# The output's bias in the dense recurrent stage: a one-row product on TensorE in place of GpSimd's addition

## What is computed

```python
def _gru_cell(x, h, wih, whh, bih, bhh):
    gi = x @ wih.T + bih
    gh = h @ whh.T + bhh
    i_r, i_z, i_n = jnp.split(gi, 3, axis=-1)
    h_r, h_z, h_n = jnp.split(gh, 3, axis=-1)
    r = jax.nn.sigmoid(i_r + h_r)
    z = jax.nn.sigmoid(i_z + h_z)
    n = jnp.tanh(i_n + r * h_n)
    return (1.0 - z) * n + z * h
...
h = jax.nn.relu(node_features @ node_proj_w.T + node_proj_b)
for l in range(L):
    ...
    h = _gru_cell(agg, h, gru_wih[l], gru_whh[l], gru_bih[l], gru_bhh[l])
    h = jax.nn.relu(h)
return h @ out_w.T + out_b
...
x = _layernorm(x + _L2_gnn_ref(x, ...), axis=-1)
```

## Time and profile before

| | us |
|---|---|
| median of 3 runs | 5060.44 |
| lowest and highest run | 5043.36, 5065.11 |
| the profiled execution | 5037.14 |
| its span, first to last instruction | 5035.4 |
| the dense recurrent stage | about 2290 to 3155 of the span |

### The profile page before, as it was taken

One profiled execution on the slowest core, in us unless ns is written; L12 is line 12 of the kernel. 1 busy time (PEld: TensorE's weight loads), 2 busy tenths in 40 slices (PEclk: granted clock), 3 DMA queues, 4 the chain that ended last, 5 costly groups with the idle time before them and its releaser, 6 DMA issues. The chain is left out here.

```text
span 5035.4 us, 61135 instructions
## 1 busy us (share of the span) xinstructions
PE 3692.6 (73%) x15176; PEld 2317.9 (46%) x15176; DVE 3382.6 (67%) x10490; ACT 2054.5 (41%) x4190; POOL 3267.5 (65%) x2884
## 2 busy tenths in 40 slices
PE   6677777774688852226999998699798758777975
PEld 4466666663344531113555554344344427665322
DVE  7878778875455543333888888465576649887964
ACT  1455555553233321115777776122222212222742
POOL 2367767774788737775888888554268867463557
PEclk9888888887899965558999999799898979899988
DMA  2344444442333321212333333333333327685863
GB/s 88 103 123 124 124 119 117 127 116 85 76 88 92 85 55 55 60 53 73 128 125 129 121 129 113 99 108 106 88 99 96 96 85 242 195 184 131 272 202 117
DMA packets 422550, 582.11 MB, mean 116 GB/s; under 512 B 69157, under 2 KB 191708, under 8 KB 422268
## 3 DMA queue, kind: packets, MB, share of 16 engines
q1 hardware_dynamic: 361660, 495.02, 31.5%
q0 software_dynamic: 54912, 83.37, 7.6%
q10 hardware_dynamic: 5696, 0.55, 0.1%
HBM read 370.70 MB, written 211.65 MB: 116 GB/s over the span
## 5 line engine op out<-in xcount | busy, mean ns | idle before, releaser
L1225 PE MATMUL ps<-big,Whh 128*128 128x512 f32 x1176 | 540.0, 595 | 33.7 <-DVE big L1243 30.4
L710 PE MATMUL ps<-W2b,hid 128*128 128x128 f32 x1568 | 260.2, 335 | 242.5 <-DVE rN L903 169.3
L1636 PE MATMUL ps<-big,We 128*128 128x512 f32 x800 | 373.0, 621 | 1.3 <-DVE agg L1810 1.1
L710 PEld LDWEIGHTS ps<-W2b,hid 128*128 128x128 f32 x1568 | 243.0, 243 | 263.4 <-issue 262.3
L1225 PEld LDWEIGHTS ps<-big,Whh 128*128 128x128 f32 x1176 | 211.8, 190 | 254.2 <-issue 251.4
L633 POOL TENSOR_TENSOR rsq<-veq,mhalf 128x8 f32<-128x8 f32 x106 | 178.9, 1688 | 201.7 <-DVE veq L942 201.4
L1784 DVE SCALAR_TENSOR_TENSOR big<-r2N,zN 128x512 f32<-128x512 f32 x400 | 258.1, 700 | 33.7 <-issue 24.1
L1258 POOL TENSOR_TENSOR big<-big 128x512 f32<-128x512 f32 x196 | 252.1, 1307 | 43.8 <-ACT big L1252 43.8
L739 ACT ACTIVATE hid<-ps 128x512 f32<-128x512 f32 x98 | 58.6, 598 | 537.4 <-PE ps L702 537.4
L599 POOL DMA_INDIRECT me<-node_tab,ix x208 | 218.9, 1052 | 70.4 <-issue 53.6
L606 POOL DMA_INDIRECT meta<-me,rank_ix x208 | 220.0, 1058 | 62.3 <-issue 61.4
(11 more groups left out here) (396 smaller groups left out, 11222.9 us busy)
## 6 DMA issues: line engine op xcount, KB each, us to landing
xN<-x_tab SPq DMA_DIRECT2D x196, 256.0 KB, 2.9
x_tab<-zN SPq DMA_DIRECT2D x189, 256.0 KB
h_tab<-yN SPq DMA_DIRECT2D x124, 256.0 KB
krow<-key_row SPq DMA_DIRECT2D x100, 256.5 KB
agg<-in_xt SPq DMA_DIRECT2D x98, 256.0 KB
agg<-x_tab SPq DMA_DIRECT2D x98, 256.0 KB
x_tab<-yN SPq DMA_DIRECT2D x93, 256.0 KB
xN<-in_x SPq DMA_DIRECT2D x65, 256.0 KB
```

Of the source, the lines that this page charges most:

```text
L710: last = nc.tensor.matmul(OUT0[:, spans[j]], hid1[g % 2][:, c, spans[j]], W2b[:, c, :], start=(c == 0), stop=(c == 1))
L1225: last = nc.tensor.matmul(bank[:, :], Whh[:, l, c * D:(c + 1) * D], h, start=True, stop=not both)
L1636: last = nc.tensor.matmul(MS[:, :], We[:, l * NTYPE + t, :], masked[g % 2][:, t, :], start=(t == 0), stop=(t == NTYPE - 1))
```

## The change

The output's bias is no longer added to x by GpSimd. For each tile of 128 rows, TensorE first forms a one-row product, 1 x 128 ones by the bias row, in the PSUM region of the output, and the product with Wo accumulates on it. VectorE's residual adds PSUM and `xR` directly. SP's second load of x into `xR` now waits for the residual that read it (`rd`), no longer for GpSimd's addition (`xbd`).

```diff
-            tpd, cpd, projd, h0d, xbd, tp1d, cp1d, yd, rd = ph.sems(9)
+            tpd, cpd, projd, h0d, tp1d, cp1d, yd, rd = ph.sems(8)
...
                     def load_again(i, q):
                         for u in range(2):
-                            free(sp, xbd, i, u=u)
+                            free(sp, rd, i, u=u)
                             sp.dma_start(xR[u], group(x2_tab, 2 * i + u)).then_inc(xagain[u], 16)
...
-                    def add_bias(i, q):
-                        for u in range(2):
-                            pool.wait_ge(xagain[u], 16 * i + 16)
-                            free(pool, rd, i, u=u)
-                            nc.gpsimd.tensor_tensor(flat(xb[u]), xR[u], flat(bo_bc), ADD).then_inc(xbd, 1)
-
...
-                        late(i, q, L5, n_pairs, add_bias)
...
-                            back_product(B, [h2[u]], [Wo[:, :]], u).then_inc(yd, 1)
+                            for j in range(J):
+                                nc.tensor.matmul(B[u][:, j * P:(j + 1) * P], ones[0:1, 0:P], bo_bc[0:1, j, :], start=True, stop=False)
+                                last = nc.tensor.matmul(B[u][:, j * P:(j + 1) * P], h2[u][:, j * P:(j + 1) * P], Wo[:, :], start=False, stop=True)
+                            last.then_inc(yd, 1)
...
                             dve.wait_ge(yd, ready(i, u))
-                            dve.wait_ge(xbd, ready(i, u))
+                            dve.wait_ge(xagain[u], 16 * i + 16)
                             free(dve, norm.done, i, u=u)
-                            nc.vector.tensor_tensor(flat(rN[u]), B[u][:, :], flat(xb[u]), ADD).then_inc(rd, 1)
+                            nc.vector.tensor_tensor(flat(rN[u]), B[u][:, :], xR[u], ADD).then_inc(rd, 1)
```

## The result

The changed kernel takes 5358.77 us (median of 4 runs, 5324.44 to 5361.73); the kernel before, run beside it, 5051.90 us (4 runs). The ratio is 1.0595, with a 95% interval from 1.0537 to 1.0652: slower by 6%, 307 us. I had forecast +349 us, 5409, in a range from 5240 to 5445. The profiled span grew from 5035.4 to 5354.6 us, by 319.2.

The account below looks back on a forecast made before the run. TensorE was taken as the bound, but for 0.70 us a round. Over 49 pairs, +192 us for one-row products and +157 us for the falling clock made +349 us: 5409 us, range 5240 to 5445 us.

Parts of the forecast that it names:

- The bound: In the final stage's steady loop, TensorE was taken to bound the kernel, but for 0.70 us a round waiting for VectorE.
- The step of 0.83 us: In TensorE's output part, one one-row product (0.41 us) plus one product with Wo (0.42); eight a pair, 6.64 us.
- The whole broken order: From output start to gates start on TensorE, alternating one-row and full weights: +3.91 us a pair, +192 us over 49 pairs.
- The Trainium skill's rule: For TensorE's output part, one-row products go out in close order, 0.11 us per record: 5107 us; rival, 3%.
- The lower end of the price: For the added one-row products on TensorE, 0.11 us per record, 3.69 less 2.73 us a pair: +47 us.
- The clock: TensorE's clock falls to half each round in the output part, for 6.8 us: 3.2 us a pair lost, +157 us.
- The rival in which the clock holds: TensorE, never idle in the new round, stays at clock 1.00: 20.6 us a pair, median 5252 us; 15%.
- SP's later load: SP's load of xR, now after the residual, costs zero; if the cover of 1.2 us fails, at most 1 us a round.
- The sum: Per pair in the final stage, 16.66 + 3.91 + 3.2 = 23.8 us; in all +349 us, median 5409 us.
- my own case: TensorE's clock falls in nearly every round: 5409 us, its own range 5375 to 5445 us, given 67%.
- the relief is worth 0.43 us a round: Without GpSimd's L1340, rstd comes sooner and VectorE's 0.43 us wait before L1166 goes; worth nothing once TensorE no longer waits.
- the rival that I gave 2%: GpSimd's relief decides, one-row products fitting into TensorE's 0.70 us of idle time: 21 us less, 5039 us; 2%.

## Why the prediction was right

**The bound** was TensorE with 0.70 us of idle time a round, and it became TensorE without any. Shown by the stretches (382.33 and 400.00 of 400 us).

**The step of 0.83 us** from the edge stage's row held to the hundredth. The whole broken order measured 3.78 us a round, with 64 rows and the clock at 1.00, against 3.91. The reason I gave, that each change between one-row and full weights breaks the close order, was right. My later extension of it to any number of rows was not: 96 rows break nothing. What sets this apart inside TensorE the runs do not show; the records say only that after each change to or from 64 or fewer rows the next two stand 0.2 us apart. The Trainium skill's rule ("TensorE: Matmul & The Clock Gate", Why this matters for your kernels: few rows take the same time) does not hold in such an alternation: by it the products would have cost what the 128-row ones did, 0.8 us a round. The lower end of the price was printed as 3.69 us; its own figures give 3.63, so +44 us, not +47, which changes nothing.

**The clock** fell in every round between 2400 and 3400 us, for 6.6 us on average against the 6.8 that I took from one spell of the edge stage. That number was a choice among rows from 3.4 to 13.7, and its closeness is in part luck. The price was 3.0 us a round, where I had 3.2. The rival in which the clock holds rested on TensorE never being idle; the run with one-row products in close order refutes it, since TensorE was busy for all of the 650 us and the clock stood at 0.83. The Trainium skill (same page, What's actually happening) says that activity releases the throttle. Read as this rival read it, that an engine which is always busy stays fast, these 650 us at 0.83 speak against it.

**SP's later load** cost nothing. In one round after, the two loads take until 2734.60, since the second waits for the second residual, and the stores go out behind them (SP's issues in order of time):

```profile
2729.51 5.09 SPq L1311 DMA_DIRECT2D agg<-x_tab  x2
```

VectorE's next L1166 was far off, in the longer round, and in the run without any bias it did not wait either.

**The sum** was 30 us too high against the span (+349, measured +319). About half is the round, 23.8 against 23.47, over 49 rounds 16 us. The rest is where I multiplied by 49: the last four rounds, in which the gates run out, cost less than the 7.1 us that I gave them: the time from one output start to the next grew by 4.5, 1.5, 3.8 and 3.0 us. In the kernel before TensorE idles there, up to 7 us at a time, so the longer work partly fell into idle time. The 5359 us lie below the range of 5375 to 5445 that I gave my own case, and within the whole range only because that reached down for the rivals' sake: the mechanism held, and the range around it was set too high.

**A wrong step that did not show** was "the relief is worth 0.43 us a round ... That is the whole of the possible gain". It measured 0.96: I took rstd's wait for the only tie between GpSimd and VectorE, and left out that the two slow each other down. It entered only the rival that I gave 2%, and there the gain would have been 47 us, not 21, still far below the cost of the products.

## What to carry to other kernels

A one-row product for a bias is not free on TensorE even in a stage with slack elsewhere: alternating with full products it took 0.61 us, not the 0.22 of its columns, and it lowered the clock for the work behind it. If a bias must go through TensorE, use all 128 rows (the identity by a tile that holds the bias in each row). Here that gave the same result for 0.8 us a round in place of 6.8, and it was still slower than leaving the addition on GpSimd. Before moving work off an engine, find the stage's bound by stretch; here the work went from an engine with 2.6 us of idle time a round to the one with 0.7.

## What the runs showed of the hardware

- A change between full weights and 64, 32 or one row puts each of the next two records 0.1 us later, in both directions: at 128 columns they stand 0.2 us apart in place of 0.11 (a step of 0.83 us). 96 rows do not (0.22 us for two records).
- The granted clock fell from 2.4 to 1.2 GHz while TensorE was busy without a gap (650 of 650 us, mean 0.83), when a part of each round consisted of one-row products. Alternating with full products, 32 rows brought it to 0.87; with 64 rows in the same order it stayed at 1.00.
- VectorE's L1166 (eight instructions from SBUF to SBUF) took 4.1 us with two additions or subtractions of GpSimd beside it and 6.0 us with four: each of these, 1.28 us long, had one L1166 beside it that took 1.31 us in place of 0.33. The two L1263 took 1.28 us alone and 2.40 beside GpSimd. L1243, which reads PSUM, kept its 0.75 us in all of them.
